# Adding four weighted corners by accumulating transposes instead of float32 products with the identity

## The chip, the cores and the metric

The kernel runs on one core of one Trainium2 chip. The metric is the device time of one launch in microseconds, taken without the profiler; three runs of the kernel before are shown. Beside them there is one profiled execution, from which every row below comes.

## The reference

The input is x, 8 images of 64 channels and 96x96 positions in float32. Four layers follow each other, each of the form x = x + layer(group_norm(x)): a linear attention over chunks of 1,024 positions (layer 0), a convolution of a deformed image (layer 1), a 3x3 convolution written as an FFT (layer 2), and a modulated deformable convolution (layer 3). The change lies in layer 3, and in the time that layer 1 takes. What they compute:

```python
# layer 1: each channel is sampled at its own offsets, then convolved
coords = conv3x3(x, W_off).reshape(b * c, h * w, 2) + grid     # clipped to the image
v_t = dy * (v_rt - v_lt) + v_lt;  v_b = dy * (v_rb - v_lb) + v_lb
out = conv3x3(dx * (v_b - v_t) + v_t, W_conv) + b_conv

# layer 3: 9 taps a position, 4 corners a tap, the same place for all 64 channels
val = g00 * (1 - wy1) * (1 - wx1) + g01 * (1 - wy1) * wx1 + g10 * wy1 * (1 - wx1) + g11 * wy1 * wx1
val = val * mask[:, None]
out = einsum('bckhw,ock->bohw', val, weight) + bias
```

## The kernel before

Two images (2 x 64 channels) make a pair, which fills the 128 partitions; there are four pairs. A program prepares pair p: layers 0, 1 and 2, and of layer 3 the offsets, the mask, the indices and the weights of the corners (written to `indices_and_weights`) and a table of pixels (`gather_table`). While it does so, it samples pair p-1: it gathers the corners of layer 3, weighs and adds them, and multiplies with the weights of the convolution. So there are three programs that do both, one that only prepares (before them) and one that only samples (after them).

Sampling goes in 36 groups a pair, each of 256 positions of both images, and a group in four steps (s = 0 to 3) of 128 positions of one image. A step runs over these engines:

- GpSimd (`pool`, L643) issues nine indirect DMAs, one a tap, which bring 4 corners x 64 channels for 128 positions into one of two buffers of `gathered_corners`. It waits until the step two before has been weighed (semaphore `weighted`).
- VectorE (`weigh`) multiplies with the weights of the corners and the mask. Where `sum_on_pe` is false it also adds the corners (L704, L707), and `sampled` holds the sum. Where it is true it only multiplies (L700), and writes four weighted corners q = 0 to 3 into the one buffer `weighted_corners` (`W`); the adding is left to TensorE.
- TensorE (`turn`) brings the 576 values of a position (9 taps x 64 channels) onto the partitions, in five blocks m of 128 (the last of 64). With `sum_on_pe` each block is four matmuls that accumulate in PSUM, with `W[:, q, block]` as the stationary operand and the identity as the moving one (L1361): the sum of four transposes, worked out as float32 products. Without it each block is one `pe.transpose` of `sampled` (L1364).
- ScalarE (`turned`, L1123 and L1124) copies the blocks from PSUM to `sampled_by_channel`.

After step 3 TensorE multiplies both images with the weights of the convolution (`project`, L1348, two times five matmuls), and VectorE's `finish` (L715) adds the bias and the residual. `finish` waits for `proj_done`, which the last of these matmuls raises.

`sum_on_pe` is true only beside the deform tiles of layer 1: 12 tiles a pair (in two loops of six), each of 8 rows, in which VectorE evaluates the bilinear sampling by weights of hat shape (L876, L879, L902, L905) and TensorE makes the offsets of the tile that follows (L1435, four banks of nine matmuls). One group of sampling goes with each tile. VectorE's order in a tile is: clip the offsets (L857 to L865), step 0, the tile's five rows of weights with step 1 after the third, step 2 after the fourth, step 3 after the last but before `finish` by way of the list `PLACES`; then `finish`, a register load of the largest offset and a branch, and the tile ends. TensorE's order in a tile is:

```python
for at in range(6):
    for gi, s in PLACES[tiles_groups[e]][at]:
        steps_of(j + G_TAPS[e], (s,))
    if at < 4 and following is not None:
        if at == 0:
            pe.wait_ge(off_read, t + 2)
        offset_bank(*following, at)
```

With `PLACES[1] = (((0, 0),), (), ((0, 1),), ((0, 2),), ((0, 3),), ((0, None),))` this is: turn 0, banks 0 and 1, turn 1, bank 2, turn 2, bank 3, turn 3, project. (In VectorE's order step 0 stands before the first row of weights, steps 1, 2 and 3 stand after the second, third and fourth of the five, and `finish` after the fifth.) All other stretches that sample call `steps_of` with `sum_on_pe=False`.

Of the kernel before, what the change touches and what calls it, by code (L numbers as in the profile page):

```python
# [112 lines left out]
def build(nc, x, Wqkv, Wout, b_out, gamma, beta, Woff, Wconv, b_conv, W2, b2, W3, b3, Wcm, bcm, out):  # L113
# [5 lines left out]
    with ExitStack() as ctx:  # L119
# [352 lines left out]
        def program(block, p, prepare, sample, ahead):  # L472
# [867 lines left out]
            def _(pe):  # L1340
# [4 lines left out]
                def project(i):  # L1345

                    for k in range(5):
                        mm = pe.matmul(ps[64 * i:64 * i + 64, 7, 0:GN], w3[:, k, :], VT[:, i, k, :], start=k == 0, stop=k == 4,  # L1348
                                       tile_position=(0, 64 * i))
                    mm.then_inc(proj_done, 1)  # L1350

                def turn(g, s, sum_on_pe):


                    pe.wait_ge(weighted, g * STEPS + (s + 1 + CREDIT))
                    pe.wait_ge(vt_copied, g * STEPS + (s + 1))
                    for m in range(5):
                        out_m = ps[:, 5, 128 * m:128 * m + 128] if m < 4 else ps[0:64, 6, 0:128]
                        if sum_on_pe:
                            for q in range(4):  # L1360
                                mm = pe.matmul(out_m, W[:, q, 128 * m:min(128 * m + 128, KK * C)], ident[:, :],  # L1361
                                               start=q == 0, stop=q == 3)
                        else:
                            mm = pe.transpose(out_m, V[:, s % 2, 128 * m:min(128 * m + 128, KK * C)], ident[:, :])  # L1364
                    mm.then_inc(transposed, 1)
                    if s == STEPS - 1:
                        pe.wait_ge(group_added, g + 1)
                        for i in range(2):
                            pe.wait_ge(vt_copied, g * STEPS + (s + 1 + i))
                            project(i)  # L1370

                def steps_of(g, steps, sum_on_pe=True):
                    if sample:
                        for s in steps:
                            if s is not None:
                                turn(g, s, sum_on_pe)
# [6 lines left out]
                with pe.Fori(0, NCHUNK) as c:  # L1383
                    pe.wait_ge(staged, c + 1)
                    for i in range(2):
                        if i == 1:
                            pe.wait_ge(y_cp, c + 1)
                        for t in range(8):
                            q = i * 8 + t
# [15 lines left out]
                    for i in range(2):  # L1405
                        pe.wait_ge(q_cp, c * 2 + (i + 1))
                        pe.wait_ge(k_norm, c * 2 + (i + 1))
                        for t in range(8):
                            q = slice(128 * (8 * i + t), 128 * (8 * i + t) + 128)
# [72 lines left out]
                with pe.Fori(0, 2) as j:  # L1482
                    for e in range(12):
                        t = j * 12 + e
                        pe.wait_ge(c2_copied, t + 1)
                        for q in range(3):
                            mm = pe.matmul(ps[0:96, e % 4, 0:RN], sum_to[:, q, :], conv_rhs(pad1_2, 1, t * ROWS, 0, 1 - q),
                                           start=q == 0, stop=q == 2)
# [3 lines left out]
                with pe.Fori(0, 2) as j:  # L1492
                    for e in range(12):
# [3 lines left out]
                                  start=True, stop=True).then_inc(c2_mm, 1)  # L1497
# [3 lines left out]
                with pe.Fori(0, 2) as j:  # L1501
                    for tile in range(12):
# [6 lines left out]
                        for k in range(5):  # L1509
                            q = k % 4  # L1510
# [96 lines left out]
```

## Time and profile before

| | us |
|---|---|
| median of three runs | 9844.04 |
| lowest and highest | 9841.66, 9857.14 |
| span of the profiled execution | 10272.1 |
| one of the three stretches of deform tiles with sampling, first to last (1972.6 to 2765) | about 793 |
| one tile in it | about 65.4 to 66.2 |

The profiled execution is 428 us longer than the median of the others. Its span is the time from the first to the last instruction. The page gives the busy time of each engine: TensorE 5575.5 us, VectorE 6423.8 us, ScalarE 2142.2 us and GpSimd 6273.4 us of the span, so that no engine is busy throughout, and stretches have to be read one by one. TensorE's mean granted clock is 0.743 of full speed: 1.0 in the rows is 2.4 GHz, and 0.5 is 1.2 GHz.

A float32 matmul stands in the trace as two MATMUL records, a transpose as one. In the timeline, neighbours of one kind are merged into one row: start, duration of the whole, engine, line, operation, out<-in, count, and in brackets the engine's idle time before it and what ended it.

### The profile page before, as it was taken

What the parts mean: (1) busy time and instruction counts of PE and PEld (TensorE: products, weight loads), DVE (VectorE), ACT (ScalarE), POOL (GpSimd) and SP (SyncE); (2) the same over time, 40 slices, a digit from 0 to 9 for tenths busy, and PEclk for the clock granted to TensorE, in tenths of its full rate; (3) what the DMA queues carried; (4) which work ended last, traced back from release to release, by engine and by line L of the source; (5) the groups of instructions that cost most, each with busy time, mean ns of one, the idle gap of its engine ahead of it and who ended that gap; (6) DMA issues with size and microseconds to landing.
All of it is one profiled execution on the core that took longest, in us unless ns stands there. A gap on an engine that the chain in (4) does not pass through costs nothing. (4 is left out here: it accounts for less than half of the span.)

```text
span 10272.1 us, 87003 instructions
## 1 busy us (share of the span) xinstructions
PE 5575.5 (54%) x26226; PEld 3400.6 (33%) x26226; DVE 6423.8 (63%) x6965; ACT 2142.2 (21%) x3640; POOL 6273.4 (61%) x5206
## 2 busy tenths in 40 slices
PE   4565766577655656577655645577655632222112
PEld 3332234355422234355422223355522211111111
DVE  5798466799845456799845456699845443333333
ACT  2343412232212112223212212233202200000000
POOL 0000047677766557677766557677767557777777
PEclk9877877788877767788876777788877765555555
DMA  2000223322324333322324323322224323333333
GB/s 67 19 0 19 65 92 97 97 77 78 97 80 122 104 97 96 98 77 76 96 79 122 106 94 94 99 77 78 94 79 123 104 85 97 97 98 97 97 98 88
DMA packets 443186, 887.37 MB, mean 86 GB/s; under 512 B 119072, under 2 KB 268918, under 8 KB 439924
## 3 DMA queue, kind: packets, MB, share of 16 engines
q0 software_dynamic: 248832, 679.81, 22.6%
q1 hardware_dynamic: 190708, 129.65, 4.3%
q10 hardware_dynamic: 3456, 75.50, 1.8%
q8 instruction: 105, 1.72, 0.1%
q14 instruction: 85, 0.70, 0.0%
HBM read 763.04 MB, written 121.53 MB: 86 GB/s over the span
## 5 line engine op out<-in xcount | busy, mean ns | idle before, releaser
L643 POOL DMA_INDIRECT gathered_corners<-gather_table,metas x5184 | 6265.2, 1209 | 3975.3 <-issue 2821.5
L702 DVE TENSOR_TENSOR gathered_corners<-gathered_corners,metas 128x2304 f32<-128x2304 f32 x432 | 1105.3, 2559 | 1774.4 <-DMA gathered_corners<-gather_table,metas 1705.3
L1364 PE MATMUL ps<-ident,sampled 128*128 128x128 f32 (+1 forms) x2160 | 496.8, 384 | 2570.7 <-DVE sampled L707 2517.6
L1123 ACT COPY sampled_by_channel<-ps 128x512 f32<-128x512 f32 x576 | 336.6, 584 | 4687.9 <-PE ps L1364 2912.1
L1364 PEld LDWEIGHTS ps<-ident,sampled 128*128 128x128 f32 (+1 forms) x2160 | 331.1, 186 | 2793.3 <-issue 2478.5
L1435 PE MATMUL ps<-region,woff 128*128 (+1 forms) x3456 | 1181.5, 498 | 23.6 <-ACT region L1108 23.6
L1361 PE MATMUL ps<-ident,weighted_corners 128*128 128x128 f32 (+1 forms) x5760 | 852.4, 316 | 253.9 <-DVE weighted_corners L700 252.1
L1361 PEld LDWEIGHTS ps<-ident,weighted_corners 128*128 128x128 f32 (+1 forms) x5760 | 808.1, 219 | 338.5 <-issue 206.4
L1435 PEld LDWEIGHTS ps<-region,woff 128*128 128x128 f32 x3456 | 654.2, 192 | 499.2 <-issue 48.6
L1348 PE MATMUL ps<-sampled_by_channel,w 128*64 128x256 f32 x2880 | 706.5, 461 | 32.8 <-ACT sampled_by_channel L1124 21.2
L876 DVE TENSOR_TENSOR work<-work 128x768 f32<-128x768 f32 x720 | 667.2, 956 | 5.0
L704 DVE TENSOR_TENSOR gathered_corners<-gathered_corners 128x1152 f32<-128x1152 f32 x432 | 586.5, 1358 | 15.0
L715 DVE SCALAR_TENSOR_TENSOR ob<-ps,chan,res 128x256 f32<-128x256 f32 x144 | 69.7, 484 | 806.3 <-PE ps L1348 370.0
L1348 PEld LDWEIGHTS ps<-sampled_by_channel,w 128*64 128x64 f32 x2880 | 405.2, 168 | 308.7 <-issue 176.6
L879 DVE TENSOR_TENSOR work<-work 128x768 f32<-128x768 f32 x540 | 499.2, 952 | 1.2
L1471 PE MATMUL ps<-region,wconv 64*64 64x384 f32 x3456 | 420.6, 566 | 99.7 <-issue 55.6
L1524 PE MATMUL ps<-region,wcm 128*64 128x384 f32 x1728 | 367.3, 524 | 77.1 <-issue 52.0
L700 DVE TENSOR_TENSOR weighted_corners<-gathered_corners,metas 128x2304 f32<-128x2304 f32 x144 | 368.4, 2558 | 33.9 <-DVE region L905 23.7
L707 DVE TENSOR_TENSOR sampled<-gathered_corners 128x576 f32<-128x576 f32 x432 | 327.6, 758 | 45.2
L1443 PE MATMUL ps<-ident,small 128*1 128x128 f32 x96 | 28.1, 396 | 558.3 <-DVE small L865 524.0
L1532 PE MATMUL ps<-work,wcs 128*64 128x384 f32 x576 | 163.3, 626 | 217.3 <-DMA work<-cosines 189.4
L1471 PEld LDWEIGHTS ps<-region,wconv 64*64 64x64 f32 x3456 | 164.8, 156 | 344.3 <-issue 295.6
(224 smaller groups left out, 7358.9 us busy)
## 6 DMA issues: line engine op xcount, KB each, us to landing
gathered_corners<-gather_table,metas POOLq DMA_INDIRECT x5184
x_after_layer<-region ACTq DMA_DIRECT2D x8, 4608.0 KB, 12.8
gather_table<-tabst SPq DMA_DIRECT2D x192, 192.0 KB
region<-in_x_dram ACTq DMA_DIRECT2D x12, 1536.0 KB, 9.6
region<-x_after_layer ACTq DMA_DIRECT2D x4, 4608.0 KB, 15.5
res<-x_after_layer SPq DMA_DIRECT2D x144, 128.0 KB
out_dram<-ob SPq DMA_DIRECT2D x144, 128.0 KB
indices_and_weights<-region SPq DMA_DIRECT2D x16, 810.0 KB
```

The costliest lines, as they stand in the source:

```text
L643: pool.indirect_dma_start(out=G[:, s % NG, k, :], out_offset=None, in_=table, in_offset=bass.IndirectOffsetOnAxis(ap=idx[:, s * KK + k:s * ...
L700: ins = ch.after().tensor_tensor(W[:].rearrange("p q (k c) -> p q k c", c=C), Gq, w4, ALU.mult)
L702: ch.own(ch.after().tensor_tensor(Gs, Gs, w.unsqueeze(2).to_broadcast([128, 4 * KK, C]), ALU.mult))
L704: ch.own(ch.after().tensor_tensor(G2[:, :, 0:2 * C], G2[:, :, 0:2 * C], G2[:, :, 2 * C:4 * C], ALU.add))
L876: return ch.own(ch.at(earlier).tensor_tensor(rows(to), rows(cx[:, q]), steps_x[:, ia:ia + DROWS, q:q + HW], ALU.mult))
L879: return ch.own(ch.at(earlier).tensor_tensor(to, to, other, op))
L1348: mm = pe.matmul(ps[64 * i:64 * i + 64, 7, 0:GN], w3[:, k, :], VT[:, i, k, :], start=k == 0, stop=k == 4, tile_position=(0, 64 * i))
L1361: mm = pe.matmul(out_m, W[:, q, 128 * m:min(128 * m + 128, KK * C)], ident[:, :], start=q == 0, stop=q == 3)
L1364: mm = pe.transpose(out_m, V[:, s % 2, 128 * m:min(128 * m + 128, KK * C)], ident[:, :])
L1435: mm = pe.matmul(ps[:, b, 0:RN], woff[:, e, k, :], conv_rhs(pad2_1, 2, j * 16 + 4 * b, k // 3 - 1, k % 3 - 1), start=k == 0, stop=k == KK - 1)
L1471: mm = pe.matmul(ps[to, b + i, 0:RN], wconv[im, k, im], rhs[im], start=k == 0, stop=k == KK - 1, tile_position=(64 * i, 64 * h))
L1524: pe.matmul(ps[64 * h:64 * h + 64, e, 0:RN], wcm[:, k, :], conv_rhs(pad1_2, 1, q * (2 * ROWS) + h * ROWS, k // 3 - 1, k % 3 - 1), start=k ...
```

## The change

In `turn`, the four matmuls of each block get `is_transpose=True`. The operands, the order, the accumulation (`start`, `stop`), the waits and the semaphores stay. It is used beside the deform tiles only, 20 matmuls a step, 4 steps a tile, 12 tiles a pair, three pairs.

```diff
                         if sum_on_pe:
                             for q in range(4):
                                 mm = pe.matmul(out_m, W[:, q, 128 * m:min(128 * m + 128, KK * C)], ident[:, :],
-                                               start=q == 0, stop=q == 3)
+                                               start=q == 0, stop=q == 3, is_transpose=True)
                         else:
                             mm = pe.transpose(out_m, V[:, s % 2, 128 * m:min(128 * m + 128, KK * C)], ident[:, :])
```

## Rows read from the trace of the kernel before

**Rows 1.** The page: busy tenths of VectorE in 40 slices of 257 us.
```profile
DVE  5798466799845456799845456699845443333333
```

**Rows 2.** Waits of VectorE (waiter <- releaser: us in total, times, longest), first stretch of tiles.
```profile
DVE ob L715 <- PE ps L1348: 18.4, 12, 2.8
DVE weighted_corners L700 <- DVE region L905: 7.9, 36, 0.2
```

**Rows 3.** The same wait in the second (line L715, idle until) and third stretch.
```profile
  PE ps L1348: 18.5, 12
DVE ob L715 <- PE ps L1348: 20.0, 12, 3.6
```

**Rows 4.** Timeline of VectorE: ends of two tiles, of the second also steps 2 and 3.
```profile
4747.81 1.02 DVE L905 TENSOR_TENSOR region<-region,work 128x768 f32 x1
4750.11 0.48 DVE L715 SCALAR_TENSOR_TENSOR ob<-ps,chan,res 128x256 f32<-128x256 f32 x1 [1.27 <-PE ps L1348]
...
4792.71 2.56 DVE L700 TENSOR_TENSOR weighted_corners<-gathered_corners,metas 128x2304 f32<-128x2304 f32 x1 [0.22 <-DVE region L905]
...
4804.30 2.56 DVE L700 TENSOR_TENSOR weighted_corners<-gathered_corners,metas 128x2304 f32<-128x2304 f32 x1 [0.22 <-DVE region L905]
4816.33 0.48 DVE L715 SCALAR_TENSOR_TENSOR ob<-ps,chan,res 128x256 f32<-128x256 f32 x1 [2.02 <-PE ps L1348]
```

**Rows 5.** Timeline of TensorE: the end of one tile, and one whole tile after it.
```profile
4741.51 4.85 PE L1361 MATMUL ps<-ident,weighted_corners 128*128 128x128 f32 x40 [0.34 <-DVE weighted_corners L700]
4746.20 3.67 PE L1348 MATMUL ps<-sampled_by_channel,w 128*64 128x256 f32 x20
...
4783.75 7.57 PE L1361 MATMUL ps<-ident,weighted_corners 128*128 128x128 f32 x40 [3.34 <-DVE weighted_corners L700]
...
4797.19 4.75 PE L1361 MATMUL ps<-ident,weighted_corners 128*128 128x128 f32 x40
4801.87 6.11 PE L1435 MATMUL ps<-region,woff 128*128 x18
4807.81 4.75 PE L1361 MATMUL ps<-ident,weighted_corners 128*128 128x128 f32 x40
```

**Rows 6.** Timeline of TensorE: transposes and non-accumulating products at full and half clock.
```profile
140.75 3.84 PE L1390 MATMUL ps<-wk,work 128*128 128x128 f32 x32 [1.04 <-DVE work L753]
...
1583.98 3.67 PE L1403 MATMUL ps<-ident,work 128*128 128x128 f32 x16 [1.09 <-ACT work L1152]
...
1938.03 0.71 PE L1364 MATMUL ps<-ident,sampled 128*128 128x128 f32 x5
```

**Rows 7.** Stretches: window, length, busy of PE, granted clock, DMA share, GB/s.
```profile
4783.70:4789.00 5.30, 5.25 (x24) 0.50 0.17 49
1584.20:1587.40 3.20, 3.20 (x16) 0.50 0.37 104
1587.80:1589.50 1.70, 1.70 (x16) 1.00 0.23 77
```

**Rows 8.** Turn 1 of tiles in the first stretch: first, longest, shortest, last of eleven.
```profile
1997.11 6.48 PE L1361 MATMUL ps<-ident,weighted_corners 128*128 128x128 f32 x40 [2.70 <-DVE weighted_corners L700]
...
2128.09 7.61 PE L1361 MATMUL ps<-ident,weighted_corners 128*128 128x128 f32 x40 [3.31 <-DVE weighted_corners L700]
...
2390.45 6.21 PE L1361 MATMUL ps<-ident,weighted_corners 128*128 128x128 f32 x40 [3.08 <-DVE weighted_corners L700]
...
2652.94 6.37 PE L1361 MATMUL ps<-ident,weighted_corners 128*128 128x128 f32 x40 [2.92 <-DVE weighted_corners L700]
```

**Rows 9.** Timeline of TensorE: project after a cold turn.
```profile
1956.80 5.17 PE L1348 MATMUL ps<-sampled_by_channel,w 128*64 128x256 f32 x20
```

**Rows 10.** Gather queue: waits in the first stretch, and two issues (VectorE busy, then idle).
```profile
POOL gathered_corners L643 <- DVE weighted_corners L700: 40.5, 12, 6.4
...
4744.24 1.43 POOL L643 DMA_INDIRECT gathered_corners<-gather_table,metas  x1 [0.31 <-issue]
4749.10 0.94 POOL L643 DMA_INDIRECT gathered_corners<-gather_table,metas  x1 [0.30 <-issue]
```

## The prediction

> **What bounds the kernel now.** I began with the page, which shows when VectorE is nearly full: its busy slices have three humps of 9 to 10 tenths, one a pair that is both prepared and sampled [rows 1]. These are the stretches of deform tiles, the only ones in which the changed line runs; everything else keeps its instructions. In such a stretch VectorE waits for TensorE at one place alone, before `finish` (L715), for the last matmul of `project` (L1348): 18.4 us in 12 tiles [rows 2], and 18.5 and 20.0 us in the other two stretches [rows 3], 56.9 us together. Its other idle time there is 0.22 us ahead of each weighing, a dependence inside VectorE (7.9 us by 36 [rows 2]). So VectorE sets the tile, and TensorE adds to it only by what `project` comes late. 56.9 us is the most that a faster TensorE could give, less a floor of 0.22 us a tile (36 tiles, 7.9 us) that stays when nothing is late: 49.0 us.
>
> The timeline shows why `project` is late. VectorE is done with step 3, works for another 7.4 us on the last row of weights and reaches L715. Meanwhile TensorE must turn step 3 and project. In the tile that ends at 4750 turn 3 starts at 4741.51, project at 4746.20, it ends at 4749.87, and L715 starts at 4750.11 [rows 4, 5]: 8.60 us after turn 3 began, where L905 had ended at 4748.83, 7.32 us after it. That makes the wait of 1.27 us. In the next tile VectorE had weighed step 3 at 4806.86, but turn 3 waited until 4807.81 for the end of bank 3, and the wait is 2.02 us [rows 4, 5]. The offsets themselves are not late: bank 3 ends near 4807.9, 8.4 us before L715.
>
> **The change, part by part.** *Fewer passes.* A turn is 40 records now, two a product, and takes 4.85 us at full clock [rows 5]. A float32 transpose of the same shape is one record: five take 0.71 us at full clock [rows 6]. A record alone takes 0.27 us to its end, so the other four add 0.11 us each, and 20 transposes come to 0.27 + 19 x 0.11 = 2.36 us. A turn gets shorter by 4.85 - 2.36 = 2.49 us at full clock.
>
> The trace has no transpose that accumulates. The nearest rows for what accumulation costs are products: 32 records that don't accumulate take 3.84 us, which is 0.115 us each after the first [rows 6], and 40 that do take 4.85 us, which is 0.117 us each [rows 5]. So I take nothing for it. The ends: 0.11 us a block, or the present 0.234 us if the accumulating form runs as the product does (no gain at all). A gain beyond 49.0 us is excluded, since VectorE waits for nothing else here.
>
> The Trainium skill's page "TensorE: Matmul & The Clock Gate" (Terms, on xbus) says that the transpose mode is four times faster for float32. The rows give 0.234 by 0.110, about twice. By the page's factor a turn would take some 1.4 us at full clock, an estimate, and the sum below would come nearer to its upper bound.
>
> *What hides it.* Turns 0, 1 and 2 of a tile are covered already: VectorE doesn't wait for them, and ScalarE's copies behind them aren't waited for either. Their gain goes into idle time of TensorE. It does one thing: bank 3 ends earlier. Turn 2 starts at once when step 2 is weighed (before, it could stand behind bank 2), 11.6 us before step 3 is [rows 4]; 2.4 us for the turn and 5.9 us for the bank leave 3.2 us in which TensorE is idle before turn 3. So the late start of turn 3 (0.95 us in the second tile of [rows 5]) is gone.
>
> *Turn 3 and project at full clock.* L715 could start 8.60 - 2.49 = 6.11 us after turn 3 begins, but L905 and the floor allow 7.32 + 0.22 = 7.54 us. TensorE would be 1.43 us early, and the whole 49.0 us would be won.
>
> *The clock takes part back.* The new idle time of 3.2 us before turn 3 is like the one that stands before turn 1 now. There the clock is still granted full when the engine falls idle, and is at half (1.2 GHz) in the turn: 0.50 for 4783.7 to 4789.0 [rows 7]. Turn 1 takes 6.21 to 7.61 us after some 3 us of idle time, in all eleven tiles that have banks beside them (the twelfth has none), instead of 4.75 us [rows 5, 8]. The extras of the eleven are 1.46 to 2.86 us: nine lie at 1.46 to 1.73 and two at 2.8. I put the same extras on turn 3 with project, which together are as long (6.0 us) as turn 1. Of each extra 1.43 us is covered; what is left is 0.03 to 0.30 us in nine tiles and 1.4 us in two, 4.9 us in eleven and 5.3 us in twelve. Wait after the change: 12 x 0.22 + 5.3 = 7.9 us a stretch, 23.9 us in three.
>
> *The sum.* 56.9 - 23.9 = 33.0 us. On the profiled execution: 10272.1 - 33.0 = 10239.1 us. That execution is 428 us longer than the median; instructions of VectorE in the tiles follow each other without gaps, so I take the tiles to be as long without the profiler and carry the gain over whole: 9844.0 - 33.0 = 9811.0 us.
>
> *Does the gain survive?* The gather queue must follow. GpSimd issues without a pause but for one wait a tile, for the weighing of step 1: 40.5 us in 12 tiles, 3.4 us each [rows 10]. A tile becomes 0.9 us shorter, and issues that fall in VectorE's idle time take 0.94 us instead of 1.43 us [rows 10]; with 0.9 us less of idle time about 0.7 issues lose 0.5 us, 0.4 us. The queue needs 1.3 of its 3.4 us. What comes after the stretch waits for VectorE's last tile and for gathers which have moved with it, so the shift should stay.
>
> **The rivals.** *A. The clock doesn't fall before turn 3*, since idle times of this length are near the edge (against it: a fall follows 2.70 us as well as 3.31 us [rows 8]). Then all is hidden: 9844.0 - 49.0 = 9795.0 us.
>
> *B. Transposes don't hold or raise the clock, and the kernel gets slower.* Place: turn 3 and project, with 20 transposes where 40 passes were. Price: at half clock 16 transposes take 3.67 us [rows 6], 0.22 us each, so a turn takes 4.6 us, and project after a cold start 5.17 us [rows 9]. L715 would come at 4.6 - 0.16 (the overlap of rows) + 5.17 + 0.24 = 9.85 us after turn 3 begins, instead of 8.60: a wait of 2.5 us a tile, 91 us in all, 34 us more than now: 9878 us. It decides where the clock costs on the average over 2.8 us a tile: the mean wait is 1.58 us now, and 1.58 + 7.32 - 6.11 = 2.79. Against it: from 1583.98 to 1587.45 TensorE ran 16 transposes and nothing else, at 0.50, and by 1587.8 it was granted 1.00, with less than half a microsecond of products behind them [rows 6, 7].
>
> The same page of the Trainium skill (Part 4, PE-mode transpose) says that the full clock doesn't engage for the transpose mode, which isn't counted as busy time in the same way. By it B would be the forecast; the rows just named disagree, so it gets a small chance.
>
> *C. The gather queue has no slack without the profiler.* The profile doesn't tell where its 428 us lie. If the queue sets the tile there, the gain is nothing, and the 0.4 us of slower issues a tile is a loss of up to 13 us: 9844 to 9857 us. For it: nothing but 0.30 us stands between two issues; against it: the wait for VectorE in every tile [rows 10].
>
> *D. The change doesn't do what it says*: accumulating transposes of float32 are run in two passes like the products, or each waits for the one before. 9844 us.
>
> **How the numbers follow.** Forecast 0.54, A 0.14, B 0.12, C 0.12, D 0.08. The predicted time is the forecast's, 9811.0 us; its own range is 9798 to 9826 (extras that all lie at 1.4 us or below, or a mean of 2.4 us). The range is 9790 to 9857: it takes in the forecast, A, C and D and leaves B out, with a little of the rest. About 0.2%, 19.7 us, is what a measurement of this kernel can tell from no change. Faster by more: A and nine tenths of the forecast, 0.63. Slower by more: B and a little of C, 0.13. The same: 0.24.
>
> **What would show it.** In the profile after: L1361 with 20 records a turn; a turn of 2.4 us at full clock and up to 4.6 us at half; turns 2 just after the weighing of step 2; an idle time of about 3.2 us before turn 3; L715's wait for L1348 at about 8 us a stretch, 2.6 us if A holds, over 25 us if B does; the wait of GpSimd for L700 smaller by some 10 to 15 us a stretch, and gone if C holds. The forecast is wrong if VectorE's wait moves to another place, such as L857 for the offsets or L700 for the gather, or if a turn takes over 3 us at full clock.

## The result and the profile after

The changed kernel takes 9813.0 us (9809.3 to 9821.5) where the kernel before takes 9844.0 us: a ratio of 0.9968, 95% interval 0.9957 to 0.9979, or 31 us less. The forecast was 9811.0 us. Where a version was run several times, its median is of the fast runs alone: one of the six runs of the version "turn 3 only, step 1 earlier" (10341 us), and one of the before runs beside it, were slow and are left out.

In the first stretch of deform tiles VectorE's wait for `project` has gone from 18.4 us [rows 2] to 8.6 us. The last line is GpSimd's wait in the same stretch, which was 40.5 us [rows 10]. Both are waits in the form of rows 2 (us in total, times, longest).

```profile
DVE work L857 <- issue: 15.9, 11, 1.5
DVE ob L715 <- PE ps L1348: 8.6, 9, 1.7
DVE weighted_corners L700 <- DVE region L905: 7.9, 36, 0.2
...
POOL gathered_corners L643 <- DVE weighted_corners L700: 29.5, 10, 4.6
```

The same wait of L715 in the second and third stretch, where rows 3 have 18.5 and 20.0 us:

```profile
DVE ob L715 <- PE ps L1348: 8.9, 10, 1.7
DVE ob L715 <- PE ps L1348: 7.8, 8, 1.8
```

The sum of the three is 25.3 us, and 56.9 us before. (The 25.3 us are 27 tiles; in the other nine L715 starts after the 0.14 us that stay when nothing is late, which this view doesn't count.) The page of the changed kernel has this group for the turns (records | busy us, mean ns of one | idle before them), with half the 5,760 records of before.

```profile
L1361 PE MATMUL ps<-ident,weighted_corners 128*128 128x128 f32 (+1 forms) x2880 | 530.3, 365 | 508.8 <-DVE weighted_corners L700 508.8
```

TensorE's timeline, to be laid beside rows 5, has turn 3 and `project` of one tile, and of the tile after it turn 1, bank 2, turn 2, bank 3, turn 3 and `project`.

```profile
2017.19 2.40 PE L1361 MATMUL ps<-ident,weighted_corners 128*128 128x128 f32 x20 [3.35 <-DVE weighted_corners L700]
2019.52 3.73 PE L1348 MATMUL ps<-sampled_by_channel,w 128*64 128x256 f32 x20
...
2058.35 4.52 PE L1361 MATMUL ps<-ident,weighted_corners 128*128 128x128 f32 x20 [6.31 <-DVE weighted_corners L700]
2062.66 6.35 PE L1435 MATMUL ps<-region,woff 128*128 x18
2070.00 2.40 PE L1361 MATMUL ps<-ident,weighted_corners 128*128 128x128 f32 x20 [0.99 <-DVE weighted_corners L700]
2072.24 6.00 PE L1435 MATMUL ps<-region,woff 128*128 x18
2081.59 4.53 PE L1361 MATMUL ps<-ident,weighted_corners 128*128 128x128 f32 x20 [3.35 <-DVE weighted_corners L700]
2086.05 4.30 PE L1348 MATMUL ps<-sampled_by_channel,w 128*64 128x256 f32 x20
```

A turn of 20 transposes takes 2.40 us at full clock. Bank 3 ends at 2078.24, step 3 is weighed at 2081.46, and TensorE stands idle for 3.35 us in between, in both tiles. In the first of them turn 3 still runs at full clock; in the second it takes 4.53 us. The stretches of the second (window, length, busy of PE, granted clock, DMA share, GB/s) show the clock full in bank 3, falling in the idle time, half in turn 3 and the first part of `project`, and full again at its end:

```profile
2075.00:2078.00 3.00, 3.00 (x10) 1.00 0.25 74
2078.30:2081.50 3.20, 0.00 (x0) 0.83 0.29 82
2081.60:2083.80 2.20, 2.20 (x11) 0.50 0.22 60
2083.90:2087.00 3.10, 3.10 (x14) 0.50 0.29 83
2087.40:2090.00 2.60, 2.60 (x18) 1.00 0.30 91
```

VectorE at the end of this tile: the weighing of step 3, and the wait before L715, where rows 4 have 1.27 and 2.02 us.

```profile
2078.90 2.56 DVE L700 TENSOR_TENSOR weighted_corners<-gathered_corners,metas 128x2304 f32<-128x2304 f32 x1 [0.22 <-DVE region L905]
...
2087.89 1.01 DVE L905 TENSOR_TENSOR region<-region,work 128x768 f32 x1
2090.60 0.48 DVE L715 SCALAR_TENSOR_TENSOR ob<-ps,chan,res 128x256 f32<-128x256 f32 x1 [1.69 <-PE ps L1348]
```

For whole stretches I take the time from the first L857 to the memset L973 that follows the last tile. In the first stretch of the changed kernel the two are these, 780.4 us apart:

```profile
1962.30 0.96 DVE L857 TENSOR_TENSOR work<-ps,neg_y 128x768 f32<-128x768 f32 x1 [0.51 <-DVE region L685]
...
2742.68 7.90 DVE L973 MEMSET work<- 96x9408 f32 x1 [3.04 <-issue]
```

The same two instructions in the profiles of all kernels of this study give the table. The idle time is VectorE's directly before L715, summed over the three stretches, with the 0.14 us that stay when nothing is late (I had put 0.22 us). Median and ratio are of the runs without the profiler; where one time was taken it has no ratio. A ratio is to the runs of the kernel before that were taken beside that version. Their median differs by up to 9 us between groups of versions: 9844.0 us beside the change; 9840.8 us beside the change again and its two parts; 9841.3 us (one run) beside the two fillings, the version without the sum and the one with eight taps; 9835.2 us beside the three with step 1 earlier. So times from different groups are not to be subtracted from each other.

| kernel | three stretches, us | idle before L715 | time, us | ratio to before |
|---|---|---|---|---|
| before | 789.8, 790.0, 792.8 | 56.9 | 9844.0 | |
| before, again | 790.0, 790.0, 792.9 | 57.6 | 9841.7 | |
| the change | 780.4, 780.6, 780.9 | 26.7 | 9813.0 | 0.9968 (0.9957 to 0.9979) |
| the change, again | 780.8, 780.8, 780.9 | 27.1 | 9814.0 | 0.9972 (0.9962 to 0.9983) |
| transposes in turn 3 only | 785.6, 785.5, 774.8 | 8.3 | 9817.5 | 0.9973 (0.9962 to 0.9984) |
| transposes in turns 0 to 2 only | 816.6, 820.3, 813.2 | 134.8 | 9915.8 | 1.0077 (1.0063 to 1.0091) |
| the change, gap filled with products | 785.4, 783.9, 774.7 | 11.5 | 9821.8 | |
| the change, gap filled with transposes | 785.5, 785.2, 775.4 | 10.2 | 9817.3 | |
| the change without the sum | 780.8, 784.7, 780.8 | 26.1 | 9815.5 | |
| turn 3 only, eight taps | 774.6, 774.6, 775.2 | 8.7 | 9370.7 | |
| turn 3 only, step 1 earlier | 776.3, 785.1, 777.0 | 17.3 | 9804.4 | 0.9967 (0.9954 to 0.9981) |
| the change, step 1 earlier | 784.7, 781.9, 772.0 | 8.4 | 9806.3 | 0.9970 (0.9959 to 0.9981) |
| before, step 1 earlier | 799.2, 797.0, 799.2 | 89.1 | 9858.6 | 1.0023 (1.0014 to 1.0033) |

From before to the change the stretches lose 9.4, 9.4 and 11.9 us, 30.7 us together, and the idle time before L715 loses 30.2 us: the whole of the measured 31 us, in the one place that the prediction named.

### The profile page after: what moved, and what is told of

Same layout as the page of the kernel before. It is cut to its first block and busy times, and to the rows that moved or that the text cites. A ratio compares the mean times of both kernels' runs of the same rounds, so it can differ in the third digit from the quotient of the medians.

```text
span 9811.3 us, 81243 instructions
## 1 busy us (share of the span) xinstructions
PE 5068.9 (52%) x23346; PEld 3040.9 (31%) x23346; DVE 6424.3 (65%) x6965; ACT 2142.6 (22%) x3640; POOL 6329.3 (65%) x5206
## 5 line engine op out<-in xcount | busy, mean ns | idle before, releaser
L1361 PE MATMUL ps<-ident,weighted_corners 128*128 128x128 f32 (+1 forms) x2880 | 530.3, 365 | 508.8 <-DVE weighted_corners L700 508.8
L1361 PEld LDWEIGHTS ps<-ident,weighted_corners 128*128 128x128 f32 (+1 forms) x2880 | 468.6, 185 | 600.6 <-issue 439.1
L715 DVE SCALAR_TENSOR_TENSOR ob<-ps,chan,res 128x256 f32<-128x256 f32 x144 | 69.7, 484 | 553.7 <-PE ps L1348 549.5
L700 DVE TENSOR_TENSOR weighted_corners<-gathered_corners,metas 128x2304 f32<-128x2304 f32 x144 | 368.4, 2558 | 33.9 <-DVE region L905 23.7
L1471 PE MATMUL ps<-region,wconv 64*64 64x384 f32 x3456 | 333.8, 545 | 44.2 <-DVEq L968 41.7
L1524 PE MATMUL ps<-region,wcm 128*64 128x384 f32 x1728 | 300.2, 492 | 0.0
L1197 ACT ACTIVATE work<-work,taps 128x768 f32<-128x768 f32 x180 | 168.4, 936 | 449.1 <-DVE work L902 310.4
L1487 PE MATMUL ps<-region,sum_to 128*96 x576 | 215.0, 532 | 24.6 <-ACT region L1108 24.6
```

The lines of the kernel that those rows point to most:

```text
L700: ins = ch.after().tensor_tensor(W[:].rearrange("p q (k c) -> p q k c", c=C), Gq, w4, ALU.mult)
```

## The experiments

**A second profile of the kernel before.** The two profiled executions differed by 461 us and the runs by 31 us, so the first profile had to be laid beside another of the same kernel. No edit.

> The kernel before, unchanged, for a second profile. Its first profiled execution lasted 10272 us where its runs took 9844 us; the profiled execution of the changed kernel lasted 9811 us. Theory: the three stretches of deform tiles (from the first L857 to the memset L973) are as long as in the first profile, 790, 790 and 793 us, and the 428 us lay elsewhere, in the convolutions and offsets after them. So the span should come near 9840 us and the waits of L715 for L1348 in the stretches should be 18 to 20 us each. Rival: the stretches themselves were stretched in the first profile, and are 9 to 12 us shorter in this one, so that the change took nothing there.

The span is 9840.0 us. The stretches are as long as in the first profile, and L715 waits 18.6, 18.7 and 20.3 us in them. What had been longer in the first profile are the parts between and behind them: 1537.9 us from the first stretch to the second, and 1395.1 us here. The loss lay outside the tiles, and the sum for the tiles stood on sound ground; the profile's span as a whole did not.

**Each part of the change alone.** Which turns are transposes was cut in two.

```diff
-                                               start=q == 0, stop=q == 3, is_transpose=True)
+                                               start=q == 0, stop=q == 3, is_transpose=s == 3)    # turn 3 only
+                                               start=q == 0, stop=q == 3, is_transpose=s < 3)     # turns 0 to 2 only
```

> Turns 0, 1 and 2 use transposes; turn 3 stays float32 products. Theory: these three give VectorE nothing, but make TensorE idle for 3.3 us before turn 3, so that turn 3 starts cold: L715 comes 8.60 us and an extra of 1.5 to 2.9 us after turn 3 begins, a wait of 1.3 + 1.9 = 3.2 us a tile instead of 1.6, 113 us instead of 57 us in the three stretches: slower than before, near 9895 us (9860 to 9910). Rival (a late bank 3 is what mattered): 5 to 9 us faster than before, 9836 us.

It is slower than before by 0.77%, 9915.8 us, a little more than the range that I gave. TensorE's timeline of a tile's end:

```profile
2285.41 7.66 PE L1361 MATMUL ps<-ident,weighted_corners 128*128 128x128 f32 x40 [3.35 <-DVE weighted_corners L700]
2292.91 3.67 PE L1348 MATMUL ps<-sampled_by_channel,w 128*64 128x256 f32 x20
```

The idle time of 3.35 us stands before turn 3, and the turn of products takes 7.66 us instead of 4.85 us. Its mean granted clock is 0.61, where it is 1.00 in the kernel before. L715 waits about 4.1 us in most tiles, 45.3 us in the first stretch. So three of the four edited turns, taken by themselves, cost 75 us (77 us of idle time before L715): they shorten work that nobody waits for, and the hole that they leave lets the clock fall under the work that is waited for. I had taken a mean extra of 1.9 us; here it was 2.8 us nearly everywhere.

> Only the turn of step 3 uses transposes; turns 0, 1 and 2 stay float32 products. Theory (only turn 3 with project is on VectorE's path, and the clock falls before turn 3 because the shorter turn 2 lets TensorE fall idle for 3.3 us): bank 3 now ends when it did before, TensorE is idle under 0.4 us before turn 3, the clock stays at 1.00 through turn 3 and project, L715 waits 0.22 us in every tile with banks, and the gain is up to 49 us: 9797 us, faster than the change with all four turns (9813). Rival (no such effect of the clock; a shorter turn anywhere helps or is neutral): the same time as the change or slower than it, 9813 to 9820 us.

Measured: 9817.5 us, not 9797. In the tiles the first half of the theory holds. Turn 3 follows bank 3 at full clock:

```profile
2340.96 6.11 PE L1435 MATMUL ps<-region,woff 128*128 128x384 f32 x18
2346.97 2.40 PE L1361 MATMUL ps<-ident,weighted_corners 128*128 128x128 f32 x20
2349.30 3.72 PE L1348 MATMUL ps<-sampled_by_channel,w 128*64 128x256 f32 x20
```

and L715 waits hardly at all (8.3 us with the floor in all three stretches). But only the third stretch became as short as that gives, 774.8 us. In the first (and the second alike) another wait took its place, VectorE's for the gather, and GpSimd's wait for VectorE is nearly gone. The group below the waits is GpSimd's issues in the stretch: count | busy us, mean ns of one | idle.

```profile
DVE weighted_corners L700 <- DMA gathered_corners<-gather_table,metas: 12.7, 7, 2.9
DVE ob L715 <- PE ps L1348: 2.3, 3, 1.2
...
POOL gathered_corners L643 <- DVE weighted_corners L700: 7.4, 2, 4.6
...
L643 POOL DMA_INDIRECT gathered_corners<-gather_table,metas x431 | 648.6, 1505 | 138.1 <-issue 130.7 <-DVE weighted_corners L700 7.4
```

An issue costs 1505 ns on the mean, and 1437 ns in the change; with 36 issues a tile that is 2.4 us of GpSimd's time a tile. This is the mechanism of my rival C, in a version where turn 3 is nearly always hidden. The time of 9817 us is also the one that the rival in the expectation names (no effect of the clock), but the rows don't bear that rival out: 30 of the 36 turns 3 run at full clock here.

> The change again, on the same chip as the two parts of it, for comparison: 9813 us, 0.3% faster than before.

As expected, 9814.0 us. The change and turn 3 alone can't be told apart by time; by their rows they are bound by different things.

**The gap before turn 3 filled.** In place of the idle time TensorE gets 2.6 to 2.8 us of work whose result nobody reads, once as products, once as transposes (the diff is against the change).

```diff
                             offset_bank(*following, at)
+                        if at == 3 and sample:
+                            for _ in range(24):    # or 11 times pe.matmul(ps[:, 4, 0:128], ident[:, :], ident[:, :], start=True, stop=True)
+                                pe.transpose(ps[:, 4, 0:128], ident[:, :], ident[:, :])
```

> The change, with 11 float32 products of the identity with itself (22 records, some 2.6 us) after bank 3, ahead of turn 3, into a bank of PSUM that nothing reads then; they fill most of the 3.3 us in which TensorE is idle before turn 3, and nothing else is altered. Theory (it is the idle time before turn 3 that lets the clock fall): turn 3 takes 2.40 us in every tile with banks, the granted clock is 1.00 through turn 3 and project, and L715 waits 0.14 us in nearly all tiles instead of 0.14 to 1.8, about 2 to 3 us a stretch instead of 9. With so little waiting the gather queue may become the bound as in the version with transposes in turn 3 alone, so the whole is expected between 9797 and 9820 us. Rival (turn 3 is slow for another reason, such as the accumulation): turn 3 still takes 4.5 us in most tiles.

> The same with 24 transposes of the identity (some 2.7 us) in place of the products. Theory (transposes hold the clock as products do): the same as with products, turn 3 at 2.40 us and L715 waiting 2 to 3 us a stretch. Rival (transposes don't count for the clock): TensorE looks idle for 5 to 6 us, the clock is at 0.50 in turn 3 and project of every tile, turn 3 takes 4.5 us and L715 waits 1.6 us or more in each, 20 us or more a stretch.

Both do the same. With transposes (L1453), in the timeline of one tile, and the clock from the last bank to `project`:

```profile
2139.45 6.00 PE L1435 MATMUL ps<-region,woff 128*128 x18
2145.29 2.78 PE L1453 MATMUL ps<-ident 128*128 128x128 f32 x24
2148.80 2.40 PE L1361 MATMUL ps<-ident,weighted_corners 128*128 128x128 f32 x20 [0.72 <-DVE weighted_corners L700]
2151.13 3.72 PE L1348 MATMUL ps<-sampled_by_channel,w 128*64 128x256 f32 x20
...
2146.00:2152.00 6.00, 5.28 (x44) 1.00 0.18 52
```

The clock stays at 1.00 through 44 transposes and into `project`, and the idle time before L715 falls from 26.7 to 10.2 us (11.5 us with products). So it was the idle time that let the clock fall, and transposes hold it as products do. The Trainium skill's page "TensorE: Matmul & The Clock Gate" (Part 4, PE-mode transpose) says that the transpose mode doesn't engage the full clock; the granted clock of these rows disagrees. The time of the kernel doesn't follow: the stretches are as in turn 3 alone (785.5, 785.2 and 775.4 us), with L700 waiting 12.8 us for the gather in the first. In the few tiles in which L700 waits for the gather the filler ends too early, TensorE idles 3.4 us again, and turn 3 is now and then slow (3.88 us at 2477.63).

**The price of accumulating.** Every transpose starts and stops its own sum, so the four corners overwrite each other; the sum of the corners is left out.

```diff
-                                               start=q == 0, stop=q == 3, is_transpose=True)
+                                               start=True, stop=True, is_transpose=True)
```

> The change with start and stop set on every transpose, so that the four corners of a block overwrite each other: the sum of the corners is left out. Measures what the accumulation costs. Theory: nothing; a turn of 20 takes 2.40 us at full clock as in the change, L715 waits 8 to 10 us a stretch, the whole 9813 us. Rival (accumulating costs something): a turn takes less than 2.3 us.

```profile
2016.22 2.40 PE L1361 MATMUL ps<-ident,weighted_corners 128*128 128x128 f32 x20 [3.35 <-DVE weighted_corners L700]
2018.55 3.73 PE L1348 MATMUL ps<-sampled_by_channel,w 128*64 128x256 f32 x20
```

A turn takes 2.40 us with and without the sum: accumulating is free. The second stretch was 784.7 us where the change has 780.6 us, with 8.1 us of idle time before L715, not more than the change. Its own waits say why: VectorE waits for the gather there.

```profile
DVE weighted_corners L700 <- DMA gathered_corners<-gather_table,metas: 6.9, 5, 2.9
```

In the change L700 never waits for the gather, and GpSimd waits 32.3 us in its second stretch where it waits 14.8 us here. So the gather queue is near to taking over even where L715 waits as in the change.

**The queue relieved.** Transposes in turn 3 alone, and GpSimd issues eight of the nine gathers of a step; the ninth tap's corners are left out. (The cut shows the loop alone; the counts of the semaphores follow it, and the buffer is zeroed once.)

```diff
-                            for k in range(KK):
+                            for k in range(KK - 1):
                                 pool.indirect_dma_start(
```

> Transposes in turn 3 alone, and GpSimd gathers eight of the nine taps (the ninth tap's corners are left out; its place in the buffer is zeroed once). It relieves the gather queue and nothing else in the tiles. Theory (with transposes in turn 3 alone L715 no longer waits, but in two of three stretches the gather queue took its place: 785.5 us each against 774.8 us in the third): all three stretches last 772 to 776 us, the wait of L700 for the gather is gone, and GpSimd waits for L700 in every tile. Rival (something else stretched the two): they stay near 785 us. The whole kernel will be much shorter since the other stretches wait for gathers; only the stretches of tiles are compared.

All three stretches are 774.6 to 775.2 us long, L700's wait for the gather is gone, and GpSimd waits for VectorE again (first stretch):

```profile
DVE ob L715 <- PE ps L1348: 1.8, 1, 1.8
...
POOL gathered_corners L643 <- DVE weighted_corners L700: 97.0, 14, 8.1
```

That settles that the queue held the two stretches of turn 3 alone at 785.5 us, and gives what is left of a stretch in this order of work once neither the queue nor turn 3 is waited for, 774.6 us.

**Step 1 placed one row of weights earlier**, in three kernels: with transposes in turn 3 alone, with the change, and with the products of before.

```diff
-          1: (((0, 0),), (), ((0, 1),), ((0, 2),), ((0, 3),), ((0, None),))}
+          1: (((0, 0),), ((0, 1),), (), ((0, 2),), ((0, 3),), ((0, None),))}
```

> Transposes in turn 3 alone, and step 1 placed one row of weights earlier (after the first of the five rows instead of the second), so that the steps of a tile are about 12.5, 21, 11.6 and 20 us apart instead of 21.8, 11.6, 11.6 and 20: with two buffers a gather must fit between a weighing and the second one after it, which is 23 us in the tightest place now and would be 31 us everywhere. Theory (once L715 no longer waits, the gather queue holds two of three stretches at 785 us because step 3's gather can't start before step 1 is weighed, 23 us before step 3): the wait of L700 for the gather shrinks, and the stretches come to 775 to 781 us each; the whole 9795 to 9808 us, faster than the change (9813) and than transposes in turn 3 alone (9817). Rival (the queue is slow for its number of issues, whatever their places): 785 us a stretch again, 9817 us.

> The change with step 1 placed one row earlier. TensorE is still idle for 3.3 us before turn 3, since steps 2 and 3 stay 11.6 us apart, so L715 should wait 8 to 9 us a stretch as in the change, and the stretches last 780 us: 9813 us. If the new place lets the clock stay up before turn 3, 2 us a stretch of waits and 9800 us.

> The kernel before with step 1 placed one row earlier, as a control for the other two: VectorE's own work sets the tile and L715's wait for turn 3 stays, so no change: 9841 us, within 5 us. Rival (the places alone are worth something): more than 10 us faster.

For turn 3 alone the theory held in two stretches (776.3 and 777.0 us); in the second the queue was still the bound, 785.1 us with L700 waiting 17.5 us for the gather. GpSimd never waits for VectorE in these stretches, so nothing is left of its slack.

With the products I had expected no change within 5 us. It is slower than before by 0.23%, and the idle time before L715 rises to 89.1 us. The rows show why. Before, the idle time of some 3 us and the slow turn behind it are those of turn 1, and turns 2 take 4.75 us [rows 8, 5]. Now banks 1 and 2 stand between turns 1 and 2, the idle time stands before turn 2, and it is turn 2 that is slow, 6.20 to 7.80 us in all 33 tiles with banks. Bank 3 comes behind it and ends late; in this tile step 3 is weighed at 2147.51:

```profile
2136.06 6.48 PE L1361 MATMUL ps<-ident,weighted_corners 128*128 128x128 f32 x40 [2.98 <-DVE weighted_corners L700]
2142.47 6.11 PE L1435 MATMUL ps<-region,woff 128*128 x18
2148.41 4.75 PE L1361 MATMUL ps<-ident,weighted_corners 128*128 128x128 f32 x40
```

Turn 3 starts 0.5 to 2.2 us after that weighing in all 33; before, it was over 0.5 us late in seven. With the change, the same move is of use. Turn 2 takes 3.73 to 4.53 us in the tiles with banks where the change has 2.40 us, and fills a part of the hole behind it. The idle time before turn 3 is 0.6 to 2.8 us instead of 3.35 us, the clock stays at 1.00 through turn 3 in 29 of 33 tiles, and the idle time before L715 is 8.4 instead of 26.7 us. I had expected the 3.3 us of idle time to stay, and so the wait. In one such tile:

```profile
2076.01 3.96 PE L1361 MATMUL ps<-ident,weighted_corners 128*128 128x128 f32 x20 [4.67 <-DVE weighted_corners L700]
2079.76 6.16 PE L1435 MATMUL ps<-region,woff 128*128 x18
2087.59 2.40 PE L1361 MATMUL ps<-ident,weighted_corners 128*128 128x128 f32 x20 [1.68 <-DVE weighted_corners L700]
```

The stretches come to 772.0 to 784.7 us, since L700 waits for the gather in the first two (16.2 and 12.0 us). Against the kernel before beside them both new versions gain 29 to 31 us, as the change does (27 to 31 us): neither is shown to beat it.

(The section on the kernel before gives VectorE's order twice. Steps 1, 2 and 3 stand after the second, third and fourth row of weights, and `finish` after the fifth, as its sentence in brackets has it; "after the third", "after the fourth" and "after the last" are wrong.)

## Why the prediction was right

**The bound.** The gain came where it was put: 30.2 us of idle time before L715, out of 31 us. TensorE's mean granted clock even fell, from 0.742 in the second profile of before to 0.727, while the kernel became faster.

**The turn.** 2.36 us was forecast from five transposes in a row [rows 6], 2.40 us was measured, and accumulation costs nothing, as the products had suggested. The page's factor of four for float32 (the Trainium skill, "TensorE: Matmul & The Clock Gate", Terms) isn't seen: 4.85 by 2.40 is two.

**The clock.** The step with most doubt was to carry the extras of turn 1 [rows 8] over to turn 3. It held: the idle time before turn 3 is 3.35 us (3.2 forecast) in each tile with banks. In the first stretch turn 3 with `project` takes 1.63 us longer than at full clock in six of the eleven tiles and 2.7 us in two, the sizes that were forecast (1.46 to 1.73 and 2.8 us). In the six the clock falls only after turn 3 has begun. In the other three it stays up; the forecast had none of these.

**What is left of the extras.** This part was sized less well. The forecast had 1.43 us of each extra covered; it is 1.16 us. From the start of turn 3 to the end of `project` it was 8.36 us and is 6.05 us at full clock, 2.31 us less and not 2.49, so that L715 could start 6.30 us after turn 3 begins, not 6.11; and the floor is 0.14 us, not 0.22. So L715's idle time is 0.61 us in the six tiles (at most 0.52 forecast, the floor with it), 1.7 us in two, 0.14 us in three, and 1.6 us in the last tile, which has no banks (0.6 forecast). Over the three stretches it is 26.7 us, against 23.9 us forecast. The total came this near in part by luck: the tiles in which the clock stayed up and the lower floor made up for most of what the smaller cover and the last tiles cost. For turns 0 to 2 alone the same carry-over was short: 2.8 us instead of 1.9 us. Why nearly every tile met so long a spell at half clock there was not tried.

**The profile's own time.** I carried the gain over whole from an execution that was 428 us too long. The second profile shows that this was allowed, and why: the excess lay between the stretches.

**The rivals.** A, the clock staying up, holds in about a quarter of the tiles. But its price, 9795.0 us, was wrong as a bound, and with it the low end of the range and the words "the whole 49.0 us would be won". The versions that nearly empty the wait, turn 3 alone and the two with the gap filled, stay at 9817 to 9822 us, since the gather queue takes over. B is refuted by the time, and its mechanism by the gap filled with transposes. C is not what holds the change: L700 never waits for the gather in its three stretches. It is what holds everything beyond the change. My reckoning of the queue, 1.3 of 3.4 us a tile used, was on the safe side for the change: GpSimd's wait in the first stretch went from 38.8 us in the second profile of before to 29.5 us, 0.8 us a tile, and an issue is no dearer (1434 and 1437 ns). It misled beyond the change, where the issues do get dearer by 2.4 us a tile. D is refuted by the 2.40 us.

## What to carry to other kernels

Before making a covered piece of TensorE's work shorter, ask what idle time that opens before the next uncovered piece: a hole of 3.35 us cost up to 2.8 us of half clock here, and the three covered turns alone made the kernel 0.77% slower. Change the piece that is waited for, and leave the ones ahead of it long or fill the hole. (Here that emptied the wait, but the kernel was no faster for it than with all four turns changed.) And a bound on a gain must be asked of the next engine as well: here a queue that waited 3 us a tile was used up before a gain of 1.3 us a tile was reached.

## What was not expected of the hardware

GpSimd's issues get dearer when the queue stops waiting. Its wait for VectorE ends with a weighing, and so lies under one; without the wait an issue stands there. Over the three stretches 113 issues still run when a weighing ends in the change, and 134 in turn 3 alone. In the timeline of turn 3 alone the issues beside the weighings at 2331.97 and 2344.35 take 2.47 and 3.26 us, where their neighbours take 1.43 us:

```profile
2331.97 2.56 DVE L700 TENSOR_TENSOR weighted_corners<-gathered_corners,metas 128x2304 f32<-128x2304 f32 x1 [0.22 <-DVE region L905]
...
2332.88 2.47 POOL L643 DMA_INDIRECT gathered_corners<-gather_table,metas  x1 [0.30 <-issue]
2335.66 1.43 POOL L643 DMA_INDIRECT gathered_corners<-gather_table,metas  x1 [0.30 <-issue]
...
2344.47 3.26 POOL L643 DMA_INDIRECT gathered_corners<-gather_table,metas  x1 [0.30 <-issue]
```

Both end 0.82 us after the weighing beside them, though they began at different times. So does every issue that still runs when a weighing ends (0.81 to 0.83 us; 106 issues before, 113 in the change, 134 in turn 3 alone). That looks like an issue which can't go on until the weighing is done, but the rows show its times alone. So losing a wait of 2.8 us does not give the queue 2.8 us. The Trainium skill's page "Advanced Engine Details and Errata" (Miscellaneous Facts, GPSIMD Details) says that GpSimd shares a read and a write interface with VectorE and conflicts with its instructions of two SBUF inputs; the weighing is one, and the trace agrees: 2.47 and 3.26 us beside it, and 0.94 us where VectorE is idle [rows 10]. Why the third stretch of turn 3 alone escaped it (774.8 us, with GpSimd waiting six times) while the first two did not was not tried: it stays open which start of the queue leads to which state.
